# Reordering the hand-written queues between attention and the routed experts: the last batch's second norm ahead of scatters, three experts' weight parts later

## What is computed

```python
x = x + _layernorm(attn(_layernorm(x)))   # 16 heads, 4 kv heads, D=128, causal, q/k layernorm, rotary
x = x + _layernorm(ffn(_layernorm(x)))

# ffn on the 2048 tokens:
probs = softmax(xf @ gate_w.T)            # 8 experts
weights, indices = top_k(probs, 2)        # renormalised to sum 1
h = silu(xf @ w_gate[e]) * (xf @ w_up[e]) # 176 wide, per expert
out = sum over the chosen e of weight * (h @ w_down[e])
out = out + sigmoid(xf @ shgate_w) * shared_mlp(xf)   # the shared expert, 352 wide, for every token
```

## Time and profile before

| | before |
|---|---|
| median of 3 runs | 674.33 us (672.16 to 675.51) |
| the profiled execution's own time | 673.56 us |
| its span, first to last instruction | 671.8 us |
| TensorE busy | 631.1 us, 94% |
| VectorE, ScalarE, GpSimd busy | 82%, 82%, 79% |
| mean granted TensorE clock | 0.991 |

### The profile page before, as it was taken

The page is one execution under the profiler, slowest core; times in us unless marked ns, Lnnn a source line. Parts: engine busy times, 40 slices in busy tenths (PEclk is TensorE's granted clock), DMA queues, the critical chain, the costliest instruction groups (busy, mean ns, idle before and its releaser), DMA issues.

```text
span 671.8 us, 15617 instructions
## 1 busy us (share of the span) xinstructions
PE 631.1 (94%) x4506; PEld 586.9 (87%) x4506; DVE 549.9 (82%) x1912; ACT 551.3 (82%) x2105; POOL 530.5 (79%) x601
## 2 busy tenths in 40 slices
PE   5879999999999999999999999999789989999993
PEld 5657899999999999999999999999678889999991
DVE  3989999898898889899898999979878755555466
ACT  3589999999999999999999999999787536666633
POOL 3698898999899899989989998999757424666664
PEclk9999999999999999999999999999899999999997
DMA  8001306997740000000000000000526033444173
GB/s 328 33 0 33 104 1 198 335 335 209 4 47 1 1 1 1 1 1 2 1 1 1 1 1 2 1 1 25 160 101 229 33 90 111 128 130 119 67 265 125
DMA packets 51122, 54.27 MB, mean 81 GB/s; under 512 B 19840, under 2 KB 42752, under 8 KB 50912
## 3 DMA queue, kind: packets, MB, share of 16 engines
q1 hardware_dynamic: 47632, 43.90, 23.6%
q0 software_dynamic: 3408, 9.38, 3.7%
HBM read 23.83 MB, written 29.51 MB: 79 GB/s over the span
## 4 chain that ended last, share of the span: by engine, by line
PE 75%; DVE 9%; POOL 5%; issue 4%; ACT 4%; DMA 2%; POOLq 0%; SPq 0%; ACTq 0%; DVEq 0%
PE pQ L470 8%; PE pQ L471 8%; PE pQ L472 8%; PE pPO L576 5%; PE pPO L470 5%; PE pPO L472 5%; PE pPO L471 5%; PE pT L548 4%; PE pSS L470 3%; PE pA L470 3%; PE pA L471 3%; PE pA L472 3%; PE pSS L471 2%; PE pSS L472 2%; POOL xs L2076 2%
## 5 line engine op out<-in xcount | busy, mean ns | idle before, releaser
L1002 ACT ACTIVATE P<-P,nmx 128x128 f32<-128x128 f32 (+1 forms) x256 | 118.8, 491 | 1.0 <-DVE nmx L1445 1.0
L470 PE MATMUL pQ<-W 128*128 128x512 f32 (+2 forms) x334 | 116.1, 347 | 2.4 <-DVE W L1359 1.2
L471 PE MATMUL pQ<-W 128*128 128x512 f32 (+2 forms) x334 | 111.6, 334 | 0.0
L472 PE MATMUL pQ<-W 128*128 128x512 f32 (+2 forms) x334 | 111.3, 333 | 0.0
L1982 POOL TENSOR_TENSOR ropes<-ropes 128x640 f32<-128x640 f32 x63 | 99.3, 1576 | 13.7 <-DVE ropes L1422 13.4
L1010 ACT ACTIVATE P<-P,rinv 128x128 f32<-128x128 f32 (+1 forms) x256 | 105.8, 481 | 2.1 <-DVE rinv L1451 2.1
L1992 POOL TENSOR_TENSOR ropes<-ropes 128x640 f32<-128x640 f32 x63 | 99.6, 1580 | 4.9
L470 PE MATMUL pPO<-W 128*128 128x256 f32 (+1 forms) x323 | 95.3, 295 | 5.6 <-DVE W L1460 3.9
L987 ACT ACTIVATE ropes<-pQ 128x128 f32<-128x128 f32 x320 | 88.4, 303 | 9.7 <-PE pQ L472 9.7
L471 PE MATMUL pPO<-W 128*128 128x256 f32 (+1 forms) x323 | 92.0, 285 | 0.0
L472 PE MATMUL pPO<-W 128*128 128x256 f32 (+1 forms) x323 | 91.8, 284 | 0.0
(11 more groups left out here) (272 smaller groups left out, 2170.5 us busy)
## 6 DMA issues: line engine op xcount, KB each, us to landing
xs<-stage SPq DMA_DIRECT2D x1, 17550.0 KB, 58.4
stage<-xs SPq DMA_DIRECT2D x39, 130.0 KB
ropes<-in_ew SPq DMA_DIRECT2D x8, 608.0 KB
stage<-in_wqkv SPq DMA_DIRECT2D x3, 768.0 KB, 9.0
stage<-ys SPq DMA_DIRECT2D x4, 512.0 KB, 7.3
ropes<-ys SPq DMA_DIRECT2D x4, 512.0 KB, 6.8
out<-X SPq DMA_DIRECT2D x7, 256.0 KB, 2.0
X<-in_wo SPq DMA_DIRECT2D x1, 1536.0 KB, 12.7
```

Source lines behind the costliest of these rows:

```text
L470: e.matmul(out, lh, rh, start=start, stop=False, skip_group_check=True)
L471: e.matmul(out, lh, rl, start=False, stop=False, skip_group_check=True)
L472: return e.matmul(out, ll, rh, start=False, stop=stop, skip_group_check=True)
L1002: a = e.activation(P[:, z, span(t)], P[:, z, span(t)], ACT.Exp, bias=nmx[:, z, t:t + 1], scale=-1.0, accum_out=sums[:, z, t:t + 1])
```

## The change

Nothing is computed in another way, and TensorE's and SyncE's lists stay as they are. Three lists are reordered. ScalarE: `ew_hi(5)` goes from behind `u_hi(1)` to behind `u_rows_hi(9)`, which itself goes ahead of `ln2_apply(7)`; `u_silu(3)` goes ahead of `u_hi(2)` and `u_out(0)`; `ew_hi(6)` and `ew_hi(7)` go behind `u_silu(8)` and `u_hi(6)`. VectorE: `ew_lo(3)` and `ew_lo(4)` go one place down each (behind `pv_lo(63)`, and behind `u_act(2)`), the parts of expert 5 behind `u_rows_lo(9)`, those of expert 6 behind `tile_list()`, those of expert 7 behind `u_lo(7)`. GpSimd: `out_root(7)` and `ln2_root(7)` each go ahead of two scatters more, and two waits on `s_uact` go.

```diff
@@ ScalarE @@
             u_hi(1)
-            ew_hi(5)
-            ew_hi(6)
+            u_silu(3)
             u_hi(2)
             u_out(0)
             u_rows_hi(7)
-            u_silu(3)
-            ew_hi(7)
             u_out(1)
             u_silu(4)
             u_rows_hi(8)
             u_silu(5)
+            u_rows_hi(9)
+            ew_hi(5)
             ln2_apply(7)
-            u_rows_hi(9)
             u_silu(6)
...
             u_silu(8)
+            ew_hi(6)
             u_out(4)
             u_hi(6)
+            ew_hi(7)
             u_out(5)
@@ VectorE @@
             ew_half(4)
+            pv_lo(63)
             ew_lo(3)
-            pv_lo(63)
-            ew_lo(4)
             u_lo(0)
             u_rows_lo(6)
             u_act(2)
+            ew_lo(4)
             out_stats(7)
             u_lo(1)
+            u_act(3)
+            u_lo(2)
+            out_scale(7)
+            out_add(7)
+            ln2_stats(7)
+            u_rows_lo(7)
+            u_act(4)
+            u_rows_lo(8)
+            u_act(5)
+            u_rows_lo(9)
             ew_half(5)
             ew_lo(5)
-            ew_half(6)
-            ew_lo(6)
-            u_act(3)
-            out_scale(7)
-            ew_half(7)
-            out_add(7)
-            ln2_stats(7)
-            u_act(4)
-            u_rows_lo(7)
-            u_rows_lo(8)
-            ew_lo(7)
-            u_lo(2)
-            u_rows_lo(9)
-            u_act(5)
             u_lo(3)
             ln2_lo(7)
...
             u_lo(6)
             tile_list()
+            ew_half(6)
+            ew_lo(6)
             u_act(8)
             u_lo(7)
+            ew_half(7)
+            ew_lo(7)
             shared_half(1, 14, NT)
@@ GpSimd @@
             scatter(1, 10, 1)
-            e.wait_ge(s_uact, 3)
+            out_root(7)
             scatter(1, 11, 0)
             scatter(1, 11, 1)
-            out_root(7)
-            e.wait_ge(s_uact, 4)
+            ln2_root(7)
             scatter(1, 12, 0)
             scatter(1, 12, 1)
-            ln2_root(7)
             scatter(1, 13, 0)
```

## The result

The changed kernel takes 679.17 us in the median of 6 runs (677.41 to 681.9), the kernel before 674.52 in 6 runs (672.16 to 675.93). The ratio is 1.0074 with a 95% interval of 1.0045 to 1.0102: 5.0 us slower (3.0 to 6.9). I had forecast 676.1 in a range of 672.6 to 678.1, so the direction was right and the size wrong, beyond the range. The profiled execution of the changed kernel took 677.41 us with a span of 675.3, 3.85 and 3.5 us more than the profiled execution before.

What follows compares the result with a forecast made beforehand. TensorE's list was taken to bound the kernel, other edits counting only through its waits. The terms summed to +1.80 us, 675.4 against the profiled 673.56, so 676.1 in the median, with an 8-in-10 range of 672.6 to 678.1.

Steps and rivals of the forecast that it cites:

- u_T(2): TensorE's step behind u_lo(1), delayed on VectorE by one low part now ahead of it: +0.30 us.
- u_down(1): TensorE waits for u_out(0), now behind u_silu(3), which needs its gate: offset +1.20 us, term +0.90.
- u_up(5): The old 1.01 us wait for u_act(4) goes and eats up the offset, leaving +0.02 us: term -1.18.
- ln2_T(7): Waits for ln2_apply(7), now behind u_rows_hi(9) and ew_hi(5) on ScalarE: offset +1.12 us, term +1.10.
- logits(7): Waits for ln2_lo(7) behind expert 5's low parts and u_lo(3) on VectorE: offset +0.97 us, term -0.15.
- u_down(5): ew_hi(6) ahead of u_out(4) on ScalarE makes TensorE 0.14 us late: offset +1.11 us.
- u_up(9): Expert 6's low parts between tile_list() and u_act(8), without slack, make a new wait: offset +2.50 us, term +1.39.
- u_T(8): The old 0.66 us wait for u_lo(7) is covered by the new wait before: offset +1.62 us, term -0.88.
- u_up(10): Waits for u_act(9) behind expert 7's low parts: offset +1.80 us, term +0.18, handed on to x_T(0).
- rival (a): TensorE's old waits of 0.48 and 1.01 us go and nothing replaces them: 672.8 us, chance 0.11.
- rival (b): Only the first half costs; expert 6's low parts fit in around the list, +0.97 stays: 675.3 us, chance 0.15.
- Rival (c): An engine stop without a releaser lands between u_rows_hi(9) and ln2_apply(7), adding 1.5 to 2.0: 677.6 to 678.1 us, chance 0.13.

Runs made afterwards that it cites:

- e2: Kernel before with only the parts of experts 6 and 7 late, on ScalarE and VectorE; ratio 0.9989 to the kernel before.
- e10: The kernel before, unchanged, profiled again on the third chip; one profile, stage 33.16 us.
- e6: Changed kernel with ew_lo(3) and ew_lo(4) back in their old places on VectorE; ratio 1.0033 to the kernel before.
- e9: The changed kernel, unaltered, run again on the third chip; ratio 1.0042 to the kernel before.
- f2: Repeat on another chip of the changed kernel with ew_lo(3) and ew_lo(4) in their old places; ratio 1.0034 to the kernel before.
- f4: The changed kernel, unaltered, run once more beside the last repeats; ratio 1.0034 to the kernel before.
- e1: Kernel before with only GpSimd's new order; ratio 1.0006 to the kernel before.
- e4: Changed kernel with expert 5's high part behind u_hi(1) and its low parts behind u_lo(1); ratio 1.0050 to the kernel before.
- e3: Changed kernel with u_silu(3) back at its old place behind u_rows_hi(7); ratio 1.0070 to the kernel before.
- e5: Kernel before with only VectorE's first edit: ew_lo(3) behind pv_lo(63), ew_lo(4) behind u_act(2); ratio 1.0004 to the kernel before.
- e8: Changed kernel with 64 more waits on a long-passed semaphore at the start of ScalarE's list; ratio 1.0039 to the kernel before.
- e11: Kernel before with experts 6 and 7 late, their low parts spread behind u_act(8), u_act(9), u_lo(8) and u_act(10); ratio 0.9973 to the kernel before.

## Why the prediction was wrong in size

The step that failed first is where the sum starts: it takes everything ahead of `u_T(2)` as unchanged, a term of nothing. In the profiled pair TensorE waits 2.67 us before `u_rows(8)` where it waited 0.17, which is +2.50, more than the whole sum of +1.80. The second is the term of the logits, forecast at -0.15 and measured at +0.29. The rest held. Step by step, "+" as in the prediction, taken from the row of after less the row of before less 0.52 us, by which `u_rows(8)` was later:

| step | forecast term | measured term |
|---|---|---|
| `u_T(2)` | +0.30 | +0.30 |
| `u_down(1)` | +0.90 | +0.94 |
| `u_up(5)` | -1.18 | -1.16 |
| `ln2_T(7)` | +1.10 | +0.99 |
| `logits(7)` | -0.15 | +0.29 |
| `u_down(5)` | +0.14 | +0.16 |
| `u_up(9)` | +1.39 | +1.46 |
| `u_T(8)` | -0.88 | -0.82 |
| `u_up(10)`, `x_T(0)` | +0.18 | +0.35 |
| sum | +1.80 | +2.51 |

**What was right.** The mechanism of every other step. `u_silu(3)` waits for its gate and takes `u_out(0)` with it; `u_up(5)` gives that back; expert 5 stands ahead of `ln2_apply(7)`; the parts of expert 6 sit in a place without slack; and rival (a), that the waits just go, fell. So did rival (b), since e2 shows the 1.30 us at `u_up(9)`. The GpSimd root did become short (1.64 to 0.73 us for its power) and this changed nothing, as the sum had it. On the three chips without the stop the time follows: +2.3 to +2.8 us against a forecast of +1.8.

**What was right by luck, in part.** The -0.88 at `u_T(8)` takes back a wait that ScalarE's stop before `u_out(6)` had made in the one profile of before. On the third chip that stop and that wait aren't there (e10), and the 0.78 us at `x_T(0)` stand in their place. And the +0.30 at `u_T(2)` is measured as forecast, but undoing its edit gives only 0.13 to 0.15 us at the end of the stage (e6 against e9, f2 against f4).

**The term that was mis-sized: `logits(7)`.** I let VectorE's parts of expert 5 start when `ew_hi(5)` ends, 528.05, and `ln2_lo(7)` end in 531.1. In the trace they start at 529.31, 0.8 us behind the end of `ew_hi(5)` at 528.51. Ahead of them stands `u_act(5)`, which waits for TensorE's `u_T(3)` (528.42, 2.61 us idle). In the list before, that wait stood in the same place ahead of `u_lo(3)` and `ln2_lo(7)`, with no 1.5 us of parts behind it. I had followed what the moved calls wait for, and not what the calls now ahead of them wait for. It is 0.44 of the missing 0.71 us; 0.17 is in the last term, and the rest in six small differences.

**What was outside the sum: ScalarE's stop.** Rival (c) named the mechanism, a stop without a releaser that lands where TensorE is waiting, with a chance of 0.13, but looked for it between `u_rows_hi(9)` and `ln2_apply(7)` and gave it 1.5 to 2.0 us from the one before `u_out(6)`. It fell before `u_hi(0)`, 3.68 us long, and TensorE's wait for it grew by 2.50. With the sum's 1.8 that is 4.3 us, 678.6 us, past the end of the range at 678.1. In the kernel before, a stop of this sort was already to be seen in the same neighbourhood: `pv_hi(63)` (L1021) started 2.09 us behind the row ahead of it, 1.2 of them behind its input. I had not counted it among them. In all twelve profiles without the stop it started 0.03 to 0.04 us behind its input.

**What stays open.** What the stop is, and whether the change sets it off. For it: in the first comparison and on the chip of e1 to e4 the three kernels that contain VectorE's new order had it before `u_hi(0)` (3.68, 2.11 and 3.65 us; in e3, with 2.11, the last 1.5 are behind its input), and the three that lack it, before, e1 and e2, had none there (0 to 0.19 us). Against it: one profile of each, and three other chips where the changed kernel had none. And the kernels that lack the new order were not free of stops there: `pv_hi(63)` came 1.24 us behind its input in before, 1.34 in e2 and 0.58 in e1, which leaves little to see at `u_hi(0)` behind it. Nor does a transfer of the instruction queue alone explain it: one of 16 KB ran just ahead of the stop (at about 508 us, 0.99 us long), and one of the same size ran at the same place in e9 (at about 505 us, 1.02 us long), where there was no stop. e5, e6, e8 and their repeats can't decide it, as they ran where it doesn't occur. It is not shown either that the timed runs of the first comparison all had it; the 5.0 us are the sum of 2.51 and 2.50 from one pair of profiles.

## What to carry to other kernels

In engines that run lists strictly in order, a call that is moved forward brings its own wait to everything that it now precedes, and a call that is moved back inherits the waits of all that now stand ahead of it: walk both, and check what the new neighbours wait for as well. Work that must be done some time before a far deadline belongs in many small free places (e11: the halves and low parts behind four different calls), not as a block behind the chain that the next stage needs (1.3 us in e2). Removing one wait is worth at most the distance to the next wait on the same path: 1.39 us at `u_down(1)` gave back 0.14.

## What the runs showed of the hardware

**Chips differ by more than the change.** The kernel before took 672.4 us in the median on the chip of e1 to e4, and 669.8, 669.4 and 669.1 on the other three; in the first comparison it was 674.5. Idle stretches of 2 to 3.7 us on ScalarE around `pv_hi(63)` and `u_hi(0)`, most of them behind a ready input, were found only where the kernel before took over 672 us.

**Executions of one program differ in TensorE's clock.** The same stretch in the profile of before, and then of after:

```profile
475.00:479.00 4.00, 3.34 (x16) 3.34 (x17) 3.08 (x10) 0.80 (x2) 3.09 (x4) 0.57 0.94 304
```

```profile
475.00:479.00 4.00, 3.63 (x25) 3.20 (x26) 3.83 (x16) 2.30 (x4) 3.08 (x4) 1.00 0.93 342
```

16 matmuls at a granted clock of 0.57 against 25 at full clock. It is in the attention, 30 us ahead of the first edit, and comes and goes between executions: the mean over 475 to 482 us is 0.55 in e10 and 1.00 in e9, and 0.54 in f4, which is the same program as e9. `u_rows(8)` started at 512.93, 509.74 and 511.70 us in these three. So the profiled spans of e10 and e9 (669.0 before, 668.4 after) say the opposite of the timed runs (1.0042), and in the first pair, where the kernel before had the low clock, the profiles differ by 3.85 us and not by 5.0. A stage measured between two later instructions of the bound engine is free of this, unless the clock drops inside it, as in e4.

**GpSimd beside VectorE.** L2023, L1966 and L1968 took 1.26, 0.38 and 1.64 us beside VectorE's low parts, and 0.23, 0.19 and 0.73 beside an idle VectorE: 2.1 us less for three instructions of 128 x 2. In e4 the last of them started 0.19 us behind `ew_half(5)` and took 0.83, so what it costs depends on the moment at which it starts. "SBUF — State Buffer" of the Trainium skill (terms and the section on its two sides) describes such a lock between VectorE operations of two SBUF inputs and GpSimd operations that read SBUF; the instruction that starts first holds it to its end. The trace agrees: the 1.64 us started 0.10 us behind an `ew_lo` of 1.16.
